# GNN layers on one core: half of the slot additions move from VectorE to TensorE and ScalarE

## Chip, cores and metric

One core of one Trainium2 chip (trn2). The metric is the device time of one execution in microseconds (us). The kernel before takes 6229.18 us, the median of three runs (6227.09, 6229.18 and 6238.08 us).

## What is computed

Four layers of a graph network (GENConv) over 6250 nodes with 64 features and 206,250 edges sorted by their destination. Cut to what matters:

```python
e = edge_attr @ enc_edge_w + enc_edge_b
def _genconv(h, e, src, dst, w1, b1, g1, bb1, w2, b2, t):
    msg = relu(h[src] + e) + EPS_MSG
    m = msg * t
    seg_max = segment_max(m, dst)
    ex = exp(m - seg_max[dst])
    denom = segment_sum(ex, dst)
    agg = segment_sum(msg * ex / (denom[dst] + 1e-16), dst)
    out = h + agg
    z = relu(_layernorm(out @ w1 + b1, g1, bb1))
    return z @ w2 + b2
# layer 0: h = _genconv(h, ...)
# layers 1 to 3: h = h + _genconv(relu(_layernorm(h, ln_g, ln_b)), ...)
```

The change concerns one sum in it: `h[src] + e`, the source's row plus the edge's encoding.

## The kernel before

A first part of some 1770 us encodes the edges and writes their encodings `e` to HBM (`ecell`), placed by destination block and slot. Then come four layers of about 1100 us. `layer` handles the nodes in 49 blocks of 128 destinations, one destination per partition. A block d has 32 slot groups for edges whose sources lie in known blocks, and V[d] overflow slots; every slot is 64 floats wide. Small and large blocks alternate: an odd d has the larger V[d] of its neighbours.

For block d the work is:

- `load_x` (L1243, SP queue): the encodings of all slots of the block into `xb[d % 2]`. It waits for `mul` of block d-2, which reads that buffer last. `load_oh` (L1250, SP queue) brings the one-hot matrices of block d.
- `gathers` (L1258): GpSimd starts V[d] indirect DMAs that bring the sources of the overflow slots into `gb[d % 2]`, after `over` of block d-2.
- `passes(d, j)` for j = 0 to 3 (L1273): TensorE picks the source rows of eight slots by one-hot products in bf16, three parts each, into PSUM bank j. All four together are 147 products of 64 columns. Before it writes a bank it waits for the addition that emptied it (`before_pass`).
- `add(d, j)` (L1290): VectorE adds bank j to the 512 columns of `xb` that hold the encodings of these eight slots, in place.
- `over(d)` (L1302): VectorE adds the gathered rows to the encodings of the overflow slots.
- `most(d)` (L1309, L1313): VectorE takes the maximum over all slots. It waits for all additions of the block.
- `sub` (L1332), the exponential on ScalarE (L1338) and `mul` (L1346): terms of the softmax, in two slices into the ring `ep`; TensorE sums each slice into one bank with products by `ident`, four slots (512 columns, float32) at a time (L1356). `fold` (L1366) reduces that bank on VectorE.
- `node_unit(u)`: for each two blocks, the division, the MLP and the two layer norms. Its steps run through VectorE, ScalarE and TensorE: L1401 hands the sum to TensorE (L1404 to L1411); the first `norm` (L243 to L263) ends in `hb`; L1419 transposes it, L1424 is ScalarE's relu, L1428 the second product, L1432 VectorE's addition to `h`; then comes the second `norm`, and L1439 and L1444 on VectorE read its result.

In `norm`, ScalarE computes the inverse root by Ln and Exp (L246, L248), each with a table load, VectorE refines it (L253, L257, L260), and ScalarE applies it (L263).

The order on every engine is the order in which the loop over d issues the work. Iteration d issues: the gathers of block d+1 on GpSimd and the loads on SP; then for j = 0 to 3 `add(d, j)`, `passes(d + 1, j)` and up to two steps of the node unit under way; `over(d)`, two steps, `most(d)`; `sub`; in an even iteration the steps L1419 to L1428; `fold(d - 1)`; in an odd iteration the start of a new node unit up to the first product; then `mul` with the sums, and further steps. So on TensorE the passes of block d+1 stand behind the sums of block d-1, and L1419 stands behind the passes. The steps of `norm` that wait for ScalarE are spaced by "gap" marks so that the additions stand between them.

At the end of a layer the new rows go to HBM (`ztab`), all engines meet, and the next layer starts. The last layer also fetches `x` rows (L1525) and scatters the output (L1460) on GpSimd.

Of the kernel before, what the change touches and what calls it, by code (L numbers as in the profile page):

```python
# [142 lines left out]
def build(nc, S, T):  # L143
    PE, VE, AE, GP, SP = nc.tensor, nc.vector, nc.scalar, nc.gpsimd, nc.sync
    ND, G = S.ND, S.G
# [5 lines left out]
    with top:  # L151
# [3 lines left out]
        pe_s, ve_s, ae_s = (next(names) for _ in range(3))  # L155
# [5 lines left out]
        def fresh():  # L161

            return Count(pe_s), Count(ve_s), Count(ae_s)
# [7 lines left out]
        def vwait(value):  # L171
            VE.wait_ge(ve_s, value)

        def awaits(engine, *tokens):
            for token in tokens:
                engine.wait_ge(*token)
# [5 lines left out]
        ident, iota, be, prow, base, full, iota1, we = (  # L182
            kept[n] for n in ("ident", "iota", "be", "prow", "base", "full", "iota1", "we"))
# [519 lines left out]
        def sorted_path():  # L703

            with ExitStack() as fc:
# [28 lines left out]
                with nc.Fori(0, S.L - 1) as i:  # L734
                    layer(i, "mid", layer_args)
                layer(S.L - 1, "last", layer_args)

        def lay(z, npd, wri, dci, outi, ovi, yc):
# [461 lines left out]
        def layer(number, tag, args):  # L1200
            (oh, z, h, npd, wri, dci, outi, ovi, xb, gb, mx, top_x, cm, ds, nt, zb, zr) = args
            final = tag == "last"
            P, V, A = fresh()
            lc = ExitStack()
            with lc:
                n_ep, ep_slots = 3, 24
                n_gp = 4
                ep = sb("ep_" + tag, [128, n_ep, ep_slots, 128], FP32, lc)
                xg = zr if final else None
                gps = bank[0:4]  # L1210
# [6 lines left out]
                xg_l = [Landed(s) for s in gq_s[6:8]]  # L1217
                xl_l = [Landed(s) for s in gq_s[8:10]]

                k = {n: {} for n in ("add", "pass", "over", "topx", "sub", "exp", "mul", "sums",  # L1220
                                     "fold", "cm", "node")}
                at = {n: {} for n in ("x", "oh", "g", "xg")}

                def x_of(d, a, b):
                    return xb[d % 2][:, 64 * a:64 * b]

                def slices(d):
                    n = -(-S.S[d] // ep_slots)
                    w = 4 * -(-S.S[d] // (4 * n))
                    return [(a, min(S.S[d], a + w)) for a in range(0, S.S[d], w)]  # L1230
# [31 lines left out]
                def passes(d, j):  # L1262

                    if j == 0 and d >= 2:
                        awaits(PE, at["oh"][d])
                    if (d, j) in before_pass:
                        PE.wait_ge(ve_s, before_pass[d, j])
                    for s in range(8 * j, min(G, 8 * j + 8)):
                        b0, n = S.groups[s]
                        for b in range(b0, b0 + n):  # L1270
                            at_oh = 128 * (S.ones[s] + b - b0)
                            for part in range(3):
                                q = PE.matmul(  # L1273
                                    gps[j % n_gp][:, 64 * (s % 8):64 * (s % 8) + 64],
                                    oh[:, d % 2, at_oh:at_oh + 128],
                                    zp[:, b, 64 * part:64 * part + 64],
                                    start=(b == b0 and part == 0),
                                    stop=(b == b0 + n - 1 and part == 2), skip_group_check=True)
                    k["pass"][d] = P(q)
                    k["pass"][d, j] = k["pass"][d]  # L1280

                before_pass = {}

                def add(d, j):
                    if j == 0 and d:
                        awaits(VE, at["x"][d])
                    VE.wait_ge(pe_s, k["pass"][d, j])
                    lo, hi = 8 * j, min(G, 8 * j + 8)
                    x = x_of(d, lo, hi)
                    k["add"][d] = V(VE.tensor_tensor(x, gps[j % n_gp][:, 0:64 * (hi - lo)], x,  # L1290
                                                     ALU.add))
                    nxt = (d, j + n_gp) if j + n_gp < JS else (d + 1, j % n_gp)
                    before_pass[nxt] = k["add"][d]

                JS = -(-G // 8)

                def over(d):
                    awaits(VE, at["g"][d])
                    if d:
                        awaits(VE, at["x"][d])  # L1300
                    x = x_of(d, G, S.S[d])
                    k["over"][d] = V(VE.tensor_tensor(x, gb[d % 2][:, 0:64 * S.V[d]], x, ALU.add))  # L1302

                def most(d):

                    vwait(max(k["over"][d], k["add"][d]))
                    if d >= 2:
                        VE.wait_ge(ae_s, k["cm"][d - 2])
                    q = V(VE.tensor_reduce(mx[:, 0:64], x_of(d, 0, S.S[d]).rearrange(  # L1309
                        "p (s f) -> p f s", f=64), AX.X, ALU.max))  # L1310
                    yield
                    vwait(q)
                    q = k["topx"][d] = V(VE.tensor_scalar(top_x[:, d % 2, :], mx[:, 0:64], 0.0,  # L1313
                                                          None, ALU.max))
                    u, i = S.where[d]
                    AE.wait_ge(ve_s, q)
                    if u >= 2:
                        AE.wait_ge(ve_s, k["node", "den"][u - 2])
                    q = A(AE.activation(cm[:, u % 2, i, :], top_x[:, d % 2, :], ACT.Exp,  # L1319
                                        scale=nt[:, 0:1]))  # L1320
                    AE.wait_ge(ae_s, q)
                    k["cm"][d] = A(AE.activation(cm[:, u % 2, i, :], cm[:, u % 2, i, :],
                                                 ACT.Identity, scale=npd[:, d:d + 1]))
# [160 lines left out]
                def store_rows(u):  # L1484

                    GP.wait_ge(ae_s, k["node", "rows"][u])
                    for i, d in enumerate(S.units[u]):
                        zs_at[u] = zs_l[u % 2](GP.indirect_dma_start(
                            T["ztab"], bass.IndirectOffsetOnAxis(ap=wri[:, d:d + 1], axis=0),
                            zb[:, u % 2, i, :], None))  # L1490
# [47 lines left out]
                awaits(PE, got_z)  # L1538
                for j in range(JS):
                    passes(0, j)  # L1540
                for d in range(ND):
# [7 lines left out]
                    for u in k["node", "rows"]:  # L1549
                        if u not in zs_at:  # L1550
                            store_rows(u)
                    for j in range(JS):
                        add(d, j)
                        if d + 1 < ND:
                            passes(d + 1, j)
                        steps(2, "normed")
# [4 lines left out]
                    for _ in most(d):  # L1561
                        steps(1, "normed")
                    ready = d and S.where[d - 1][0] != S.where[d][0]
                    steps(99, "end" if ready else "turned")
                    n = len(slices(d))
# [483 lines left out]
```

## Time and profile before

| | |
|---|---|
| Median of three runs | 6229.18 us |
| Profiled execution, its time | 6223.69 us |
| Its span, first to last instruction | 6219.3 us |
| Before the first layer | about 1770 us |
| Mean granted TensorE clock | 0.823 |
| TensorE matmul busy | 4569.7 us |
| VectorE busy | 4590.5 us |
| ScalarE busy | 2451.0 us |
| GpSimd busy | 4260.6 us |

In the rows PE is a TensorE matmul, PEld a TensorE weight load, DVE is VectorE, ACT is ScalarE, POOL is GpSimd and SPq is the queue of SyncE. L1290 is line 1290 of the kernel. A time in brackets behind "idle before" is idle time of that engine right before the instruction, with what ended it. Busy time of DMA-issuing instructions on SP is not counted.

### The profile page before, as it was taken

Reading aid. Unit: us, or ns where it says so; the run is one execution under the profiler, and the core shown is the slowest. Engines: PE = TensorE matmul, PEld = TensorE weight load, DVE = VectorE, ACT = ScalarE, POOL = GpSimd, SP = SyncE. Lnnn points to the kernel's source line nnn. Section 1 sums busy time; section 2 is a strip of 40 time slices with the busy share of each in tenths; the row PEclk is TensorE's granted clock in tenths of the full one; section 3 lists DMA queues with packets and bytes.
Section 4 is the critical chain, followed back from the end, with each engine's and each line's share of the span. In section 5 each row is a group of like instructions: output and inputs, shape, how many; then the busy total and the mean of one; then the engine's idle time right before and its main releaser. Section 6 shows DMA issues by size and latency. Waiting matters only on the chain. (4 is left out here: it accounts for less than half of the span.)

```text
span 6219.3 us, 106998 instructions
## 1 busy us (share of the span) xinstructions
PE 4569.7 (73%) x43557; PEld 3223.3 (52%) x43557; DVE 4590.5 (74%) x7210; ACT 2451.0 (39%) x3848; POOL 4260.6 (69%) x3850
## 2 busy tenths in 40 slices
PE   6715788989937877883877788478878856777776
PEld 6705777888824544452444454245444534444443
DVE  9432555444438999994899999389999948988887
ACT  3403666555513444441334444133443423433333
POOL 3054777766557777774777777477777747777775
PEclk9956988666668998896899889689988978888887
DMA  9962777665565555544555555445555544555452
GB/s 365 416 218 81 255 277 270 230 246 214 190 186 174 177 180 172 185 156 119 169 174 184 176 175 175 119 149 177 180 169 183 183 132 136 172 167 172 158 168 87
DMA packets 323285, 1168.13 MB, mean 188 GB/s; under 512 B 142130, under 2 KB 145380, under 8 KB 255444
## 3 DMA queue, kind: packets, MB, share of 16 engines
q1 hardware_dynamic: 172852, 890.91, 39.1%
q0 software_dynamic: 134800, 214.63, 13.8%
q10 hardware_dynamic: 15120, 55.50, 2.2%
q8 instruction: 352, 5.77, 0.4%
q14 instruction: 161, 1.32, 0.1%
HBM read 910.82 MB, written 249.92 MB: 187 GB/s over the span
## 5 line engine op out<-in xcount | busy, mean ns | idle before, releaser
L1258 POOL DMA_INDIRECT gb<-ztab,ovi x2704 | 2991.3, 1106 | 1009.7 <-issue 826.9
L1356 PE MATMUL bank<-ep_mid,keep 128*128 128x512 f32 (+3 forms) x3474 | 1579.0, 613 | 18.5 <-DVE ep_mid L1346 18.5
L1356 PEld LDWEIGHTS bank<-ep_mid,keep 128*128 128x128 f32 x3474 | 703.8, 204 | 859.3 <-issue 830.2
L1309 DVE TENSOR_REDUCE mx<-xb 128x64 f32<-128x2816 f32 (+17 forms) x196 | 1018.1, 5195 | 3.6
L1273 PE MATMUL bank<-zpw,oh_layers 128*128 128x64 bf16 x28812 | 879.8, 194 | 155.4 <-DMA zpw<-ztab 155.4
L1273 PEld LDWEIGHTS bank<-zpw,oh_layers 128*128 128x128 bf16 x28812 | 874.5, 98 | 210.7 <-DMA zpw<-ztab 156.5
L1096 POOL DMA_INDIRECT ecell<-zpw,ptg x588 | 646.7, 1100 | 227.6 <-issue 177.7
L1404 PE MATMUL bank<-keep,na 128*128 128x128 f32 x100 | 47.5, 475 | 963.1 <-DVE na L1401 963.1
L925 PE MATMUL bank<-byk,zpw 88*88 88x102 f32 (+13 forms) x4608 | 649.5, 327 | 57.8 <-DVE zpw L906 54.1
L925 PEld LDWEIGHTS bank<-byk,zpw 88*88 88x88 f32 (+13 forms) x4608 | 638.0, 229 | 68.9 <-DVE zpw L906 60.3
L1319 ACT ACTIVATE cm<-top_x,nt 128x64 f32<-128x64 f32 x196 | 68.2, 348 | 1505.5 <-DVE top_x L1313 1505.5
L906 DVE TENSOR_TENSOR zpw<-keep,kct 88x440 f32<-88x440 f32 (+13 forms) x468 | 285.3, 631 | 467.4 <-PE bank L925 464.1
L1290 DVE TENSOR_TENSOR xb<-bank,xb 128x512 f32<-128x512 f32 x784 | 510.2, 684 | 107.0 <-PE bank L1273 82.1
L1356 PE MATMUL bank<-ep_last,keep 128*128 128x512 f32 (+3 forms) x1158 | 533.9, 620 | 6.2 <-DVE ep_last L1346 6.2
L1404 PEld LDWEIGHTS bank<-keep,na 128*128 128x128 f32 x100 | 18.2, 182 | 975.4 <-DVE na L1401 975.4
L1338 ACT ACTIVATE ep_mid<-ep_mid,pack 128x1280 f32<-128x1280 f32 (+10 forms) x327 | 444.8, 1390 | 174.9 <-DVE ep_mid L1332 171.7
L1332 DVE SCALAR_TENSOR_TENSOR ep_mid<-xb,top_x 128x1280 f32<-128x1280 f32 (+10 forms) x327 | 484.2, 1527 | 8.8 <-DVE top_x L1313 1.4
L1346 DVE SCALAR_TENSOR_TENSOR ep_mid<-xb,ep_mid 128x1280 f32<-128x1280 f32 (+10 forms) x327 | 489.5, 1524 | 0.5 <-ACT ep_mid L1338 0.5
L1356 PEld LDWEIGHTS bank<-ep_last,keep 128*128 128x128 f32 x1158 | 237.1, 207 | 291.5 <-issue 282.7
L844 ACT COPY bys<-bank 88x325 f32<-88x325 f32 (+11 forms) x468 | 198.6, 424 | 474.6 <-PE bank L925 471.1
L1302 DVE TENSOR_TENSOR xb<-gb,xb 128x768 f32<-128x768 f32 (+17 forms) x196 | 210.5, 1074 | 207.8 <-DMA gb<-ztab,ovi 207.7
L844 ACT COPY byk<-bank 88x512 f32<-88x512 f32 (+10 forms) x306 | 316.0, 1158 | 28.0 <-PE bank L885 27.8
(222 smaller groups left out, 5816.5 us busy)
## 6 DMA issues: line engine op xcount, KB each, us to landing
oh_layers<-ohd SPq DMA_DIRECT2D x196, 1568.0 KB, 9.8
ea_in<-in_ea SPq DMA_DIRECT2D x101, 512.0 KB, 8.4
enc<-es_out ACTq DMA_DIRECT2D x101, 512.0 KB
cb<-rowc SPq DMA_DIRECT2D x49, 1024.0 KB, 5.7
gb<-ztab,ovi POOLq DMA_INDIRECT x2704
ohd<-oh_lay SPq DMA_DIRECT2D x49, 576.0 KB
xb<-ecell SPq DMA_DIRECT2D x20, 1408.0 KB
ohd<-oh_lay SPq DMA_DIRECT2D x49, 512.0 KB
```

The lines of the kernel that those rows point to most:

```text
L844: k["ev"][m] = A(AE.copy(to, src(bank[4 + m % 4])))
L906: k["hot"][g] = V(VE.tensor_tensor(hot[0:kp, g % 3, 0:n, 0:mp], iota1[0:kp, None, 0:mp].broadcast_to([kp, n, mp]), kct[0:kp, a:a + n][:, : ...
L925: q = PE.matmul(b[0:mp, WIDE * j:WIDE * j + WIDE], hot[0:kp, g % 3, j, 0:mp], byk[0:kp, at_d:at_d + WIDE], start=True, stop=True)
L1096: at["sc"][j, h] = sc_l[h](GP.indirect_dma_start(T["ecell"], bass.IndirectOffsetOnAxis(ap=ptg[:, j % 2, e:e + 1], axis=0), prows[:, h, a:a ...
L1258: at["g"][d] = ga_l[d % 2](GP.indirect_dma_start(gb[d % 2][:, 64 * v:64 * v + 64], None, T["ztab"], bass.IndirectOffsetOnAxis(ap=ovi[:, i: ...
L1273: q = PE.matmul(gps[j % n_gp][:, 64 * (s % 8):64 * (s % 8) + 64], oh[:, d % 2, at_oh:at_oh + 128], zp[:, b, 64 * part:64 * part + 64], sta ...
L1290: k["add"][d] = V(VE.tensor_tensor(x, gps[j % n_gp][:, 0:64 * (hi - lo)], x, ALU.add))
L1309: q = V(VE.tensor_reduce(mx[:, 0:64], x_of(d, 0, S.S[d]).rearrange("p (s f) -> p f s", f=64), AX.X, ALU.max))
L1332: k["sub"][d, i] = V(VE.scalar_tensor_tensor(ep[:, r, 0:b - a, 64:128], x_of(d, a, b).rearrange("p (s f) -> p s f", f=64), 0.0, top_x[:, d ...
L1338: k["exp"][d, i] = A(AE.activation(ep[:, r, 0:b - a, 0:64], ep[:, r, 0:b - a, 64:128], ACT.Exp, scale=tcol))
L1346: k["mul"][d, i] = k["mul"][d] = V(VE.scalar_tensor_tensor(ep[:, r, 0:b - a, 64:128], x_of(d, a, b).rearrange("p (s f) -> p s f", f=64), 0 ...
L1356: q = PE.matmul(both[d % 2][:, 0:w], ident, rows[:, 128 * (c - a):128 * (c - a) + w], start=(c == 0), stop=(c + 4 >= S.S[d]), skip_group_c ...
```

## The change

For j = 2 and 3 (`summed`), the passes of a bank begin with a product of `ident` and the 512 columns of encodings in `xb`, in float32, which starts the bank; the one-hot products then accumulate on it. TensorE waits for the load of that block's encodings first. The result is copied back over the encodings in `xb` by ScalarE (the new list `lift`), and VectorE does no addition for these two banks. A bank is free for its next passes when that copy has ended. `most` additionally waits for the last copy of its block. For j = 0 and 1 nothing changes.

```diff
                     if (d, j) in before_pass:
-                        PE.wait_ge(ve_s, before_pass[d, j])
-                    for s in range(8 * j, min(G, 8 * j + 8)):
+                        PE.wait_ge(*before_pass[d, j])
+                    lo, hi = 8 * j, min(G, 8 * j + 8)
+                    if j in summed:
+                        if d:
+                            awaits(PE, at["x"][d])
+                        PE.matmul(gps[j % n_gp][:, 0:64 * (hi - lo)], ident, x_of(d, lo, hi),
+                                  start=True, stop=False, skip_group_check=True)
+                    for s in range(lo, hi):
...
-                                    start=(b == b0 and part == 0),
+                                    start=(b == b0 and part == 0 and j not in summed),
...
                 def add(d, j):
                     if j == 0 and d:
                         awaits(VE, at["x"][d])
-                    VE.wait_ge(pe_s, k["pass"][d, j])
                     lo, hi = 8 * j, min(G, 8 * j + 8)
                     x = x_of(d, lo, hi)
+                    nxt = (d, j + n_gp) if j + n_gp < JS else (d + 1, j % n_gp)
+                    if j in summed:
+                        AE.wait_ge(pe_s, k["pass"][d, j])
+                        k["lift"][d] = A(AE.copy(x, gps[j % n_gp][:, 0:64 * (hi - lo)]))
+                        before_pass[nxt] = ae_s, k["lift"][d]
+                        return
+                    VE.wait_ge(pe_s, k["pass"][d, j])
                     k["add"][d] = V(VE.tensor_tensor(x, gps[j % n_gp][:, 0:64 * (hi - lo)], x,
                                                      ALU.add))
-                    nxt = (d, j + n_gp) if j + n_gp < JS else (d + 1, j % n_gp)
-                    before_pass[nxt] = k["add"][d]
+                    before_pass[nxt] = ve_s, k["add"][d]
 
                 JS = -(-G // 8)
+                summed = (2, 3)
...
                     vwait(max(k["over"][d], k["add"][d]))
+                    VE.wait_ge(ae_s, k["lift"][d])
```

## Rows read from the trace of the kernel before

**Rows 1.** The page's busy times, whole span

```profile
PE 4569.7 (73%) x43557; PEld 3223.3 (52%) x43557; DVE 4590.5 (74%) x7210; ACT 2451.0 (39%) x3848; POOL 4260.6 (69%) x3850
```

**Rows 2.** Busy time by engine in a stretch; the second layer

```profile
2870.00:3970.00 1100.00, 814.76 (x8686) 506.20 (x8686) 938.32 (x1365) 418.46 (x657) 800.43 (x721) 0.86 0.51 164
```

**Rows 3.** VectorE's waits (us, times, longest): second layer, then last layer

```profile
DVE h L1432 <- PE bank L1428: 36.1, 25, 3.8
DVE xb L1302 <- DMA gb<-ztab,ovi: 34.3, 1, 34.3
...
DVE xb L1302 <- DMA gb<-ztab,ovi: 112.0, 20, 34.9
```

**Rows 4.** Groups of instructions by line, whole span

```profile
L1356 PE MATMUL bank<-ep_mid,keep 128*128 128x512 f32 (+3 forms) x3474 | 1579.0, 613 | 18.5 <-DVE ep_mid L1346 18.5
L1290 DVE TENSOR_TENSOR xb<-bank,xb 128x512 f32<-128x512 f32 x784 | 510.2, 684 | 107.0 <-PE bank L1273 82.1 <-DMA xb<-ecell 13.1 <-issue 11.8
L844 ACT COPY byk<-bank 88x512 f32<-88x512 f32 (+10 forms) x306 | 316.0, 1158 | 28.0 <-PE bank L885 27.8
L301 ACT COPY es_out<-bank 128x512 f32<-128x512 f32 x202 | 108.5, 589 | 183.6 <-PE bank L293 164.0 <-DMA enc<-es_out 19.7
```

**Rows 5.** Timeline of blocks 28 to 31, second layer: start, duration, engine, line

```profile
3507.30 4.45 PE L1273 MATMUL bank<-zpw,oh_layers 128*128 128x64 bf16 x147
3513.15 9.45 PE L1356 MATMUL bank<-ep_mid,keep 128*128 128x512 f32 x22
3513.35 0.29 DVE L1432 TENSOR_TENSOR h<-h,bank 128x128 f32<-128x128 f32 x1 [1.22 <-PE bank L1428]
3515.87 0.32 SPq L1243 DMA_DIRECT2D xb<-ecell  x1
3517.34 0.16 DVE L257 SCALAR_TENSOR_TENSOR nwf<-nwf 128x2 f32<-128x2 f32 x1
3518.01 0.15 DVE L260 SCALAR_TENSOR_TENSOR nwf<-mv,nwf 128x2 f32<-128x2 f32 x1
3519.01 0.29 DVE L1439 TENSOR_TENSOR na<-hb,pack 128x128 f32<-128x128 f32 x1 [0.24 <-ACT hb L263]
3520.88 5.52 DVE L1309 TENSOR_REDUCE mx<-xb 128x64 f32<-128x3072 f32 x1
3522.44 4.45 PE L1273 MATMUL bank<-zpw,oh_layers 128*128 128x64 bf16 x147
3534.13 0.29 DVE L1401 TENSOR_TENSOR na<-na,z 128x128 f32<-128x128 f32 x1
3536.45 11.94 PE L1356 MATMUL bank<-ep_mid,keep 128*128 128x512 f32 x24
3540.20 0.20 ACT L248 ACTIVATE nwf<-nwf 128x2 f32<-128x2 f32 x1
3540.44 0.35 DVE L253 SCALAR_TENSOR_TENSOR nwf<-nwf 128x1 f32<-128x1 f32 x2
3542.49 4.84 DVE L1309 TENSOR_REDUCE mx<-xb 128x64 f32<-128x2752 f32 x1
...
3548.23 4.45 PE L1273 MATMUL bank<-zpw,oh_layers 128*128 128x64 bf16 x147
3554.29 0.29 DVE L1432 TENSOR_TENSOR h<-h,bank 128x128 f32<-128x128 f32 x1 [1.26 <-PE bank L1428]
```

**Rows 6.** Stretches: busy PE, PEld, DVE, ACT, POOL; granted clock; DMA share; GB/s

```profile
3524.00:3525.00 1.00, 1.00 (x40) 1.00 (x37) 1.00 (x1) 0.00 (x0) 0.70 (x2) 1.00 0.04 10
...
3529.00:3530.00 1.00, 0.00 (x0) 0.00 (x0) 1.00 (x2) 0.23 (x1) 1.00 (x1) 0.59 0.83 339
...
3913.00:3917.00 4.00, 0.00 (x0) 0.00 (x0) 4.00 (x4) 3.29 (x3) 0.00 (x0) 0.74 0.00 0
```

**Rows 7.** GpSimd's waits (us, times, longest), second layer

```profile
POOL gb L1258 <- DVE zb L1464: 17.9, 8, 7.3
...
POOL gb L1258 <- DVE xb L1302: 3.7, 1, 3.7
```

More of the change, by code:

```diff
@@ L1218, in layer @@
                 xl_l = [Landed(s) for s in gq_s[8:10]]
-                k = {n: {} for n in ("add", "pass", "over", "topx", "sub", "exp", "mul", "sums",
+                k = {n: {} for n in ("add", "lift", "pass", "over", "topx", "sub", "exp", "mul", "sums",
                                      "fold", "cm", "node")}
```

## Prediction

> **What bounds the kernel now.** I read the page's busy times first. VectorE is busy 4590 us and TensorE 4570 us of 6219 [rows 1]: two engines are equally full, so no share tells which one a piece of work should be taken from. The first 1770 us are untouched by the change. In one layer VectorE is busy 938 of 1100 us, TensorE 815 and GpSimd 800 [rows 2]. VectorE looks like the bound, but its waits say where it is not: in each of 25 node units it stops at L1432 for TensorE's L1428, 36.1 us per layer [rows 3]. The decisive view is the timeline of two neighbouring blocks, which repeats 23 times in a layer [rows 5]. It splits into two halves.
>
> *Half B*, from L1432 at 3513.35 to the end of L1401 at 3534.42: 21.07 us. VectorE runs here almost without a break. TensorE does the sums (9.45 us), then the 147 passes (4.45), and is through at 3526.89; it then idles 7.6 us until L1401 hands it the node sum.
>
> *Half A*, from 3534.42 to the next L1432 at 3554.29: 19.87 us. TensorE does the node's products, the sums of the larger block (11.94 us from 3536.45), the passes from 3548.23 to 3552.68, then L1419, and after ScalarE's L1424 the product L1428. VectorE needs that result and has waited 1.26 us. So half A is TensorE's: whatever is put into its queue ahead of L1419 delays L1432, and only half B is VectorE's.
>
> **The change, part by part.**
>
> *Removed:* two of four additions per block at 0.684 us [rows 4], 1.37 us per block of VectorE, 2.74 per pair, 268 us over 196 blocks.
>
> *Added on TensorE:* two identity products of 512 float32 columns per block. The trace has the same kind in the sums: 43 slots make 11 products, shown as 22 records in 9.45 us [rows 5], so 0.43 us per record and 0.86 per product. (The 613 ns of [rows 4] is the length of one record; records overlap, so the spacing is the price.) Two are 1.72 us per block. They stand in the passes, which take the same 4.45 us in both halves, at the full clock of half B's (1.00 [rows 6]). The bounds: 1.7 us where all is hidden but the stream, 1.9 with a float32 weight load that the short bf16 products ahead can't hide. I take 1.72.
>
> *In half A* these 1.72 us lie on the path to L1432 (the passes of the next block stand ahead of L1419): +1.72 us. What VectorE gains in this half comes to nothing, since it arrives earlier at the same wait. That gain is small anyway: L253 waits for ScalarE's L248, which ends at 3540.40 [rows 5], whether three additions or two stand ahead of it.
>
> *In half B* the 1.72 us come ahead of TensorE's 7.6 us of idle time, which shrinks to about 5.4: cost nothing. If that cover went, the next late thing would be L1404. VectorE drops two additions. The chain of the second norm needs them as cover: L257 ends at 3517.50; L260 followed at 3518.01 because an addition stood between, and can now follow at about 3517.54. L1439 came 1.00 us after L260 because it waits for ScalarE's L263 [rows 5]; the addition that stood in this gap goes, and the gap stays. So L1439 and all behind it come 0.47 us earlier, not 1.37. Bounds: 0.2 if a copy delays L263, 1.37 if the gap could be filled. I take 0.47.
>
> *Added on ScalarE:* two copies out of PSUM per block. The nearest row is L301, same shape, 0.589 us; the helper's copies at L844, with 88 partitions and strided output, took 1.16 [rows 4]. I take 0.59. In block order one copy stands behind L248 and the next ahead of or behind L263. In half B the second copy ends near 3519.1 (L1439's old start), and `most`, the first to need it, started at 3520.88 and can now at 3520.4: hidden, even at 1.16 us. In half A the copies follow L248 and end at 3540.40 + 1.18 = 3541.6, before `most` at 3542.49 less up to 0.5: hidden too, and at 1.16 us up to 0.8 us late, which falls into VectorE's wait at L1432. Over the layer ScalarE goes from 418 us busy by 58 us.
>
> *New waits.* TensorE waits for the load of the encodings at its third bank. In half A the load is issued after the two `mul` that follow L1401, some 10 us before the passes begin. In half B it is issued at 3515.87; the DMA engines are empty by 3524 (share 0.04) [rows 6]; the third bank would start after 51 of 147 passes, 3522.44 + 1.54 = 3523.98. This is tight, but a stall here of up to 5 us falls into TensorE's idle time. The wait of the passes for the copies of the block before is met 4 us or more earlier in both halves. SP and GpSimd issue nothing new and stand behind no new wait; the gathers of block d+1 still wait for `over` of d-1. VectorE's wait for the last copy is costed above.
>
> *Clock.* In the idle time of half B the granted clock falls from full to half (2.4 to 1.2 GHz) after 2.3 us (0.59 in 3529 to 3530 [rows 6]), and the first sums of half A run at half rate. With 5.4 us idle I expect the same fall: in the shorter idle stretch of 4.2 us near 3913 it fell too (mean 0.74 [rows 6]). So no gain and no loss.
>
> *Sum.* Per pair +1.72 − 0.47 = +1.25 us. Half A with passes behind its sums occurs in blocks 2, 4, ... 46: 23 per layer, and half B as often. Three layers: 69 × 1.25 = +86 us. At a layer's start the extra products are hidden by the one long wait for the gathered rows of block 1 (34.3 us [rows 3]). In the last layer VectorE waits 20 times for the gathered rows (112.0 us [rows 3]), GpSimd having more to issue there: about 4 to 5 us per pair from block 13 on, which swallows both the 1.25 us of each pair and the 7 us gathered before. I take 0 for it; bounds 0 to +8.
>
> The sum is made on the profiled execution, 6223.7 + 86 = 6310 us; the median of the runs stands 5.5 us above it, so 6315 us.
>
> **The rivals.**
>
> *R1, VectorE bounds throughout: faster.* If L1432's wait could be absorbed elsewhere, each pair would gain up to 2.74 us, 63 per layer. GpSimd caps this: within a layer it waits only 17.9 + 3.7 us for VectorE [rows 7], otherwise it issues without a break, so a layer can't shrink by more than some 25 us. Time: 6229 − 3 × 25 = 6154 us. For it speaks VectorE's larger busy time; against it, the 25 waits at L1432. It decides if TensorE's half A is 1.3 us or more shorter than I read it. Chance 0.08.
>
> The Trainium skill (Perfetto Trace Analysis, "Identifying the Most-Contended Engine") would have one find the engine with the highest occupancy and relieve it first. By that VectorE is relieved and the time falls as in R1. The waits in this case's trace speak against it.
>
> *R2, the clock stays up: slightly faster.* If 5.4 us of idle time with a load's stall in it no longer lets the clock fall, half A's sums run at 0.43 us per record from the start: 24 × 0.43 = 10.3 instead of 11.94 us, −1.6 per pair. Net −0.35 × 69 = −24: 6205 us. Against it, the fall after 2.3 us. Chance 0.05.
>
> The Trainium skill (TensorE: Matmul & The Clock Gate, "Loop structure matters more than you think") says that back-to-back matmuls keep the clock up and long waits lose it. A denser TensorE queue would by this rule lean to R2; the 4.2 us row says that this change is not dense enough.
>
> *R3, no change.* The addition to half A is offset by 1.2 us: L1424 and L1428 close up, or the pair's rhythm falls well against the clock. Time 6229. Chance 0.05.
>
> *R4, slower by more.* The lifted products run at the half clock (1.72 more), or the copies delay L263 and so L1439, or the load stalls TensorE beyond its idle time. One of them per pair adds about 0.8 to 1.7 us: 69 × 2.0 to 3.0 = 138 to 207, 6367 to 6436 us. Against it: half A's passes now take no longer than half B's, and half B has cover. Chance 0.10.
>
> **How the numbers follow.** My case has 0.72. Its own ends: +0.35 per pair (B gains 1.37) gives 24 us, 6253; 1.9 on TensorE and 0.2 gained, with 8 in the last layer, gives 125 us, 6354. The range needs 8 in 10, so it goes up a little into R4: 6250 to 6370. A measurement can tell about 0.2% (12 us) from no change. Faster: R1 and R2, 0.13. Same: R3, 0.05. Slower: my case and R4, 0.82.
>
> **What would show it.** Right: L1290 ×392; VectorE's wait at L1432 grows from 1.5 to about 3.4 us each in the first three layers, about +45 us per layer; TensorE's passes last about 6.2 us; the wait of L1439 for ScalarE grows to about 0.9; the two-block period goes from 40.9 to about 42.2 us in the first three layers and stays about 44 late in the last, with shorter waits for gathered rows. Wrong: waits at L1432 that stay near 1.2 us, a clock that doesn't fall between L1273 and L1404, or VectorE waiting for gathered rows in the middle layers, which would be GpSimd as the new bound.

## Result and profile after

The changed kernel takes 6320.59 us (median of four runs, 6313.32 to 6323.0) against 6228.14 us: a ratio of 1.0151, 95% interval 1.0128 to 1.0175, so 92 us slower. The prediction was 6315 us.

The page's busy times of the changed kernel (in the order of [rows 1]):

```profile
PE 4941.6 (78%) x44340; PEld 3369.7 (53%) x44341; DVE 4368.9 (69%) x6818; ACT 2629.8 (42%) x4240; POOL 4294.0 (68%) x3850
```

VectorE lost 222 us of work and the kernel became slower. The new groups by line; L1272 is the identity product, L1298 ScalarE's copy, L1302 the addition that stays:

```profile
L1272 PE MATMUL bank<-xb,keep 128*128 128x512 f32 x784 | 449.3, 656 | 133.4 <-DMA xb<-ecell 132.4
...
L1302 DVE TENSOR_TENSOR xb<-bank,xb 128x512 f32<-128x512 f32 x392 | 252.2, 684 | 101.7 <-PE bank L1279 85.8 <-DMA xb<-ecell 15.9
...
L1298 ACT COPY xb<-bank 128x512 f32<-128x512 f32 x392 | 214.3, 572 | 213.5 <-PE bank L1279 213.5
```

VectorE's waits in the second layer of the changed kernel (us in total, times, longest), to be read against [rows 3]. L1445 is the old L1432, L1314 the old L1302, L1452 the old L1439:

```profile
DVE h L1445 <- PE bank L1441: 83.3, 25, 5.6
DVE xb L1314 <- DMA gb<-ztab,ovi: 40.2, 3, 39.3
...
DVE na L1452 <- ACT hb L263: 21.0, 25, 0.8
DVE nwf L253 <- ACT nwf L248: 18.0, 26, 1.8
```

The wait for TensorE's L1441 rose from 36.1 to 83.3 us. That growth of 47 us exceeds the loss of a layer, some 25 us: it contains what VectorE gained by arriving earlier. The timeline of the same blocks as in [rows 5] shows both halves. L1279 is the passes (three pieces of 51, 48 and 48), L1369 the sums, L1414 the old L1401:

```profile
3569.54 0.29 DVE L1445 TENSOR_TENSOR h<-h,bank 128x128 f32<-128x128 f32 x1 [4.18 <-PE bank L1441]
...
3578.62 1.65 PE L1279 MATMUL bank<-zpw,oh_layers 128*128 128x64 bf16 x51
...
3580.94 1.10 PE L1272 MATMUL bank<-xb,keep 128*128 128x512 f32 x2 [0.67 <-DMA xb<-ecell]
...
3589.62 0.29 DVE L1414 TENSOR_TENSOR na<-na,z 128x128 f32<-128x128 f32 x1
...
3591.64 11.88 PE L1369 MATMUL bank<-ep_mid,keep 128*128 128x512 f32 x24
...
3595.93 0.35 DVE L253 SCALAR_TENSOR_TENSOR nwf<-nwf 128x1 f32<-128x1 f32 x2 [0.59 <-ACT nwf L248]
...
3603.36 1.65 PE L1279 MATMUL bank<-zpw,oh_layers 128*128 128x64 bf16 x51
3604.85 1.10 PE L1272 MATMUL bank<-xb,keep 128*128 128x512 f32 x2
3605.79 1.56 PE L1279 MATMUL bank<-zpw,oh_layers 128*128 128x64 bf16 x48
3607.19 1.10 PE L1272 MATMUL bank<-xb,keep 128*128 128x512 f32 x2
3608.13 1.56 PE L1279 MATMUL bank<-zpw,oh_layers 128*128 128x64 bf16 x48
3611.30 0.29 DVE L1445 TENSOR_TENSOR h<-h,bank 128x128 f32<-128x128 f32 x1 [3.21 <-PE bank L1441]
3616.47 0.29 DVE L1452 TENSOR_TENSOR na<-hb,pack 128x128 f32<-128x128 f32 x1 [0.84 <-ACT hb L263]
```

The two halves as stretches (columns as in [rows 6]):

```profile
3569.54:3589.91 20.37, 15.57 (x173) 9.07 (x172) 18.21 (x31) 8.89 (x16) 16.11 (x15) 1.00 0.60 205
3589.91:3611.30 21.39, 20.89 (x189) 11.91 (x190) 17.28 (x22) 9.68 (x15) 17.12 (x15) 0.92 0.45 144
```

Half B went from 21.07 to 20.37 us, half A from 19.87 to 21.39. In half A TensorE is busy 20.89 of 21.39 us. The passes last from 3603.36 to 3609.69, 6.33 us in place of 4.45.

Over the 69 pairs of the first three layers in which half A has passes, worked out from the starts of the two additions to `h` and the ends of the node sums: half A grew by 1.6 us on average (20.1 to 21.7), half B shrank by 0.5 (21.2 to 20.7). From block 1's maximum to block 48's a layer takes 996 to 1004 us (971 to 975 before). That is 77 of the 96 us that part the two profiled executions. The last layer's blocks add 3.5, the edges of the layers 3. The other 12 us lie ahead of the first layer, in code that the change doesn't touch: the first gather starts at 1761.2 instead of 1748.9. In the profiled executions of these two kernels and of the first four experiments it lies between 1748.0 and 1761.2, and one kernel with the products starts as early as the kernel before; so the change is not needed for a late start. Whether the other three executions of the changed kernel have these 12 us too was not recorded.

### The profile page after: what moved, and what is told of

Same layout as the page of the kernel before. It is cut to its first block and busy times, and to the rows that moved or that the text cites. A ratio compares the mean times of both kernels' runs of the same rounds, so it can differ in the third digit from the quotient of the medians.

```text
span 6315.7 us, 108957 instructions
## 1 busy us (share of the span) xinstructions
PE 4941.6 (78%) x44340; PEld 3369.7 (53%) x44341; DVE 4368.9 (69%) x6818; ACT 2629.8 (42%) x4240; POOL 4294.0 (68%) x3850
## 5 line engine op out<-in xcount | busy, mean ns | idle before, releaser
L1258 POOL DMA_INDIRECT gb<-ztab,ovi x2704 | 3033.5, 1122 | 1063.5 <-issue 828.7
L1369 PE MATMUL bank<-ep_mid,keep 128*128 128x512 f32 (+3 forms) x3474 | 1555.8, 606 | 0.0
L1279 PEld LDWEIGHTS bank<-zpw,oh_layers 128*128 128x128 bf16 x28812 | 938.9, 99 | 446.3 <-issue 274.8
L1369 PEld LDWEIGHTS bank<-ep_mid,keep 128*128 128x128 f32 x3474 | 692.5, 202 | 829.0 <-issue 794.2
L1279 PE MATMUL bank<-zpw,oh_layers 128*128 128x64 bf16 x28812 | 954.0, 194 | 156.2 <-DMA zpw<-ztab 156.2
L1272 PE MATMUL bank<-xb,keep 128*128 128x512 f32 x784 | 449.3, 656 | 133.4 <-DMA xb<-ecell 132.4
L1369 PE MATMUL bank<-ep_last,keep 128*128 128x512 f32 (+3 forms) x1158 | 523.2, 610 | 0.6 <-DVE ep_last L1359 0.6
L1369 PEld LDWEIGHTS bank<-ep_last,keep 128*128 128x128 f32 x1158 | 232.5, 203 | 279.4 <-issue 267.2
L1314 DVE TENSOR_TENSOR xb<-gb,xb 128x768 f32<-128x768 f32 (+17 forms) x196 | 210.8, 1075 | 202.5 <-DMA gb<-ztab,ovi 202.3
```

Of the source, the lines that this page charges most:

```text
L1258: at["g"][d] = ga_l[d % 2](GP.indirect_dma_start(gb[d % 2][:, 64 * v:64 * v + 64], None, T["ztab"], bass.IndirectOffsetOnAxis(ap=ovi[:, i: ...
L1272: PE.matmul(gps[j % n_gp][:, 0:64 * (hi - lo)], ident, x_of(d, lo, hi), start=True, stop=False, skip_group_check=True)
L1279: q = PE.matmul(gps[j % n_gp][:, 64 * (s % 8):64 * (s % 8) + 64], oh[:, d % 2, at_oh:at_oh + 128], zp[:, b, 64 * part:64 * part + 64], sta ...
L1369: q = PE.matmul(both[d % 2][:, 0:w], ident, rows[:, 128 * (c - a):128 * (c - a) + w], start=(c == 0), stop=(c + 4 >= S.S[d]), skip_group_c ...
```

## Experiments

The first four ran against a kernel before of 6226.3 us (median of 13). Lines in the expectations are those of the kernel before, L1314 excepted.

**Only even blocks, only odd blocks.** The rule that picks the banks looks at the block too; both kernels compute all of it.

```diff
-                summed = (2, 3)
+                def lifts(d, j):
+                    return d % 2 == 0 and j in (2, 3)   # second kernel: d % 2 == 1
```

> Only even blocks take the identity products and the copies. Their passes are issued in odd iterations, ahead of TensorE's idle time (half B), and their copies fall into half A, where VectorE waits for TensorE anyway. My theory (the products cost only where they stand ahead of L1419 in half A, VectorE gains only in half B): 0 +- 10 us against the kernel before, 6228, and the wait at L1432 of the second layer grows only by what VectorE gains, from 1.5 to about 1.9 us each. Rival, the cost is spread over all products (slower engines through more work on TensorE and ScalarE): half of the change's loss, +46. Rival, VectorE's removed additions count wherever they are: -25 to -50.

> Only odd blocks take the products and the copies. Their passes stand in half A, ahead of L1419 (+1.72 us per pair), their copies in half B (-0.47). My theory: the whole loss of the change, +86 to +92, so 6314 to 6320. Rival, the cost is spread evenly: +46.

Measured: even 6218.19 us (0.9982, interval 0.9972 to 0.9991), odd 6310.11 us (1.0137, 1.0118 to 1.0156). Nearly the same number of products, copies and removed additions (24 blocks of a layer are odd, 25 even) costs 84 us in one place and gains 8 in the other. This rules out a cost spread over all products, and it rules out VectorE's removed additions as a gain wherever they are. The profiled executions agree: blocks 1 to 48 of the first three layers together take 72 us longer with odd blocks and 4.5 us less with even ones. VectorE's wait for the second product in the second layer (36.1 us before), even blocks, then odd:

```profile
DVE h L1448 <- PE bank L1444: 45.9, 25, 3.8
```

```profile
DVE h L1448 <- PE bank L1444: 73.1, 25, 5.6
```

With even blocks it grows by 9.8 us (0.4 each), what VectorE gains in half A and can't use. With odd ones half A is 1.5 us longer and half B 0.5 shorter, close to the changed kernel. The even kernel is also a little faster than the kernel before, at the edge of what can be told. Its blocks 1 to 48 take 0.8 us more in the first layer and 2.3 and 3.0 less in the next two; the profiled execution is the slowest of its ten (6227.4 us), so where the 8 us are gained is not shown.

**The product left out.** The encodings of 16 of the 32 slot groups are not added; the wait for the load and the copies stay.

```diff
-                        PE.matmul(gps[j % n_gp][:, 0:64 * (hi - lo)], ident, x_of(d, lo, hi),
-                                  start=True, stop=False, skip_group_check=True)
...
-                                    start=(b == b0 and part == 0 and j not in summed),
+                                    start=(b == b0 and part == 0),
```

> As the changed kernel, but the identity product is left out: the encodings of 16 of the 32 slot groups are not added, TensorE does the 147 products alone (its wait for the load stays), ScalarE copies as before. My theory: TensorE's +1.72 us in half A goes, VectorE's -0.47 in half B stays: -32 us, 6196. The wait at L1432 stays near 1.9 us. If VectorE were the bound throughout: -75 (GpSimd then caps it). If the copies or the new waits were the cost and not the product: it stays near 6310.

Measured: 6256.15 us (1.0044, 1.0027 to 1.0061). 64 us less than the changed kernel, but 30 more than before, where 32 less were expected. Half A did return to 20.1 us (before 20.1). Half B did not stay short: it takes 21.6 us (before 21.2). The rest is a bound that I had put too far away. VectorE's waits in its second layer:

```profile
DVE xb L1312 <- DMA gb<-ztab,ovi: 57.2, 9, 38.2
DVE h L1443 <- PE bank L1439: 51.2, 25, 3.8
```

VectorE waits for gathered rows nine times instead of once. Up to block 29 the layer gained 3.6 us on the kernel before; from there to block 48 it lost 13. The gathers themselves were slower: a gather of blocks 2 to 48 took 1.14 us on average in this layer, 1.11 before, 17 us over 637 of them. The traces show where. A gather takes 0.94 us (the median) while no `scalar_tensor_tensor` of VectorE runs, and 1.26 on average (up to 2.51) in the kernel before when it meets one. But this is not what changed: in the second layer gathers and these instructions coincide for 273 us, 274 before. What changed is the meeting with the overflow addition, L1312 here, whose two operands both lie in SBUF. Before, 52 gathers of the layer overlap it and take 1.01 us on average; here 66 do, and take 1.23. Above 0.94 each, that is 15 of the 17 us. One of them:

```profile
3084.82 1.48 DVE L1312 TENSOR_TENSOR xb<-gb,xb 128x1280 f32<-128x1280 f32 x1
...
3085.22 1.90 POOL L1258 DMA_INDIRECT gb<-ztab,ovi  x1 [0.30 <-issue]
```

The changed kernel has 54 such gathers of 1.18 us on average. Fewer additions on VectorE let the overflow addition start earlier, but that this alone makes more gathers fall into it, and that the slower gathers are all of the 30 us, is argued and not shown.

**Copies by VectorE.**

```diff
-                        AE.wait_ge(pe_s, k["pass"][d, j])
-                        k["lift"][d] = A(AE.copy(x, gps[j % n_gp][:, 0:64 * (hi - lo)]))
-                        before_pass[nxt] = ae_s, k["lift"][d]
+                        VE.wait_ge(pe_s, k["pass"][d, j])
+                        k["add"][d] = V(VE.tensor_copy(x, gps[j % n_gp][:, 0:64 * (hi - lo)]))
+                        before_pass[nxt] = ve_s, k["add"][d]
...
-                    VE.wait_ge(ae_s, k["lift"][d])
```

> As the changed kernel, but VectorE makes the copies out of PSUM in place of ScalarE: VectorE then has as many instructions of the same shape as before, and TensorE the added products. My theory: +1.72 us per pair from TensorE and nothing gained in half B: 69 x 1.72 = +119, 6347; if a copy is shorter than the 0.684 us addition by a tenth, some 5 us less. Rival, ScalarE's copies are a cost of the change (they delay L263 or the maximum): then this is no slower than the changed kernel, 6320 or less.

Measured: 6335.07 us (1.0181, 1.0159 to 1.0204), 109 us slower than before, where 119 were expected. VectorE's copies by line, to be read against L1302 in the groups above (684 ns):

```profile
L1298 DVE COPY xb<-bank 128x512 f32<-128x512 f32 x392 | 266.2, 682 | 37.8 <-PE bank L1279 31.6 <-issue 6.2
```

A copy costs VectorE as much as the addition. Half B is back at 21.1 us (20.7 in the changed kernel, 21.2 before) and half A stays at 21.7. So half B's gain comes from taking the work off VectorE, and ScalarE's copies cost nothing that these halves show; the intervals of this kernel and of the changed one overlap, so it is the halves and not the totals that show it.

**A period of slower execution.** The runs that follow fell, on three chips, one of them the chip of the four runs above, into a time in which the kernel before took 8404 to 8580 us. So each is compared only with the kernel before that ran beside it. The traces show TensorE stopping within the passes for no wait that they name ("issue"). TensorE's largest wait from 2300 us on, in the kernel of the next paragraph with the fourth group:

```profile
PE bank L1279 <- issue: 1387.6, 2106, 60.0
```

What stopped it is not known. In that kernel half A takes 37 us and half B 21 in the first three layers: TensorE's passes weigh much more than in the profile of before. The kernel before itself has no trace from this period.

**One slot group at a time.** `j in (2, 3)` becomes `j == 3`, and `j == 2`.

> Only the fourth slot group (j = 3) of every block. TensorE +0.86 us in half A. VectorE's fourth addition stood between L260 and L1439, where VectorE waits for ScalarE's L263 for 1.00 us anyway, so taking it out gains nothing: 0. My theory: 69 x 0.86 = +59 us, 6287, and the wait at L1439 goes from 0.24 to about 0.9 us. Rival, each removed addition gains its 0.684 us in half B: +0.18 per pair, +12.

> Only the third slot group (j = 2) of every block. TensorE +0.86 us in half A; the third addition stood between L257 and L260, so L260 comes 0.47 us earlier, and the fourth addition still fills the wait for L263. My theory: 69 x 0.39 = +27 us, 6255. Both banks gain alike if it is not the place in the norm's chain that counts: then the same time as with the fourth group alone.

Measured: fourth group 8467.52 us (1.0064, 1.0029 to 1.0099), third 8438.72 us (1.0022, 0.9993 to 1.0051), before 8413.42. The order is as expected (the fourth costs more, 54 and 25 us by the medians, 59 and 27 forecast), but the intervals overlap, and the times alone don't decide. VectorE's wait for the second norm does. In the second layer, fourth group, then third (L1455 is the old L1439):

```profile
DVE na L1455 <- ACT hb L263: 21.0, 25, 0.8
```

```profile
DVE na L1455 <- ACT hb L263: 7.2, 25, 0.8
```

In the profile of before this wait was 7.2 us too. Without the fourth addition it grows to 0.84 us each (0.9 forecast); without the third it stays at 0.24, and half B is 0.45 us shorter than with the fourth removed. So it is the place in the norm's chain that counts: the time that the fourth addition gives back goes into the wait, and half B's gain comes from the third.

**Later passes.** In even iterations the passes of the next block leave the places ahead of L1419. All outputs are computed.

```diff
-                        if d + 1 < ND:
+                        if d + 1 < ND and d % 2:
                             passes(d + 1, j)
...
                     steps(99, "end" if ready else "turned")
+                    if d + 1 < ND and d % 2 == 0:
+                        for j in (0, 1):
+                            passes(d + 1, j)
                     n = len(slices(d))
                     for i in range(n):
                         sub(d, i)
                     steps(99, "linear2")
+                    if d + 1 < ND and d % 2 == 0:
+                        for j in (2, 3):
+                            passes(d + 1, j)
```

Applied to the kernel before:

> The kernel before, with one order changed: in even iterations the passes of the next block are issued behind L1419 (two banks) and behind L1428 (two banks), no longer ahead of both. My theory: TensorE's half A ends 4.45 us sooner, L1432 no longer waits, and half A becomes VectorE's: -1.2 us per pair, more in blocks 2 to 10 where the wait was up to 3.8: about -34 us per layer of the first three, but GpSimd's gathers cap it at some -25: -60 to -90 in all, about 6155. If the wait at L1432 had another cause (ScalarE's part), no change.

Measured: 7905.65 us against 8413.42 (0.9415, 0.9376 to 0.9454). Applied to the changed kernel:

> The changed kernel with the same later passes in even iterations. The two added products no longer stand ahead of L1432, so half A costs nothing for them and VectorE's shorter work counts in both halves (-0.45 and -0.47). My theory: at least as fast as the kernel before with the same order, 6135 to 6155, held there by GpSimd's gathers, with VectorE waiting at the overflow addition (L1314) in the later half of every layer. TensorE's idle time in half B nearly vanishes (7.6 - 4.6 - 1.7 and less), so the clock may stay up. Rival, the products cost wherever they stand (TensorE total, 36 of 39 us per pair): 6228 or more.

Measured: 7985.22 us (0.9505, 0.9468 to 0.9543). Both were run twice more.

> Again the kernel before with its passes of even iterations behind L1419 and L1428, after a run on a chip where every kernel takes a third longer. On a chip like that of the profile, my theory: the wait at L1432 (36 us per layer before) shrinks to below 15, and the time falls by what GpSimd's gathers allow. The kernel without the product showed them as the next bound, so less than I took for this at first: -20 to -70 us, 6155 to 6205. If the wait at L1432 is not TensorE's queue: 6226.

> Again the changed kernel with the later passes. My theory: the products stand in TensorE's idle time in both halves, the loss of the change (+92) goes, and the time is that of the kernel before with the same order within 20 us, held by GpSimd's gathers. Rival, TensorE's total counts: it stays 60 us or more above the kernel before with the same order.

> The kernel before with its passes of even iterations behind L1419 and L1428, tried a third time for a chip on which the kernel before takes some 6226 us. There: the wait at L1432 shrinks to below 15 us per layer and the time falls by 20 to 70 us, to 6155 to 6205, held by GpSimd's gathers; 6226 if the wait at L1432 is not TensorE's queue. On a chip like the last two: 0.943 of the kernel before again.

> The changed kernel with the later passes, the same. Where the kernel before takes 6226 us: within 20 us of that kernel with the same order, as the products then stand in TensorE's idle time; rival, TensorE's total counts, and it stays 60 us or more above it. On a chip like the last two: 0.951 again, so some 60 us above.

Measured: 7934.4 (0.9430, 0.9382 to 0.9477) and 7996.06 us (0.9509, 0.9464 to 0.9553) against 8404.25; 8151.0 (0.9512, 0.9467 to 0.9556) and 8219.53 us (0.9582, 0.9531 to 0.9633) against 8579.89. The slower period lasted, so how much the order gains outside it, the 20 to 70 us expected, was not measured. In it the last pair gained less than the 0.943 and 0.951 expected of it.

What they show is the mechanism. VectorE's waits for the second product from 2300 us on, in the kernel with the fourth group alone (passes ahead of it), and in the kernel before with later passes ("remote" is a releaser that the trace doesn't name):

```profile
DVE h L1448 <- PE bank L1444: 687.4, 90, 15.4
```

```profile
DVE h L1432 <- PE bank L1428: 73.9, 87, 4.3
...
DVE h L1432 <- remote: 47.1, 13, 10.2
```

Passes that no longer stand ahead of it bring this wait from 687 to 121 us (the two kernels also differ by the fourth group's product). The kernel with the products is 62 to 80 us slower than the one without, in the same order. By the times, then, my expectation (within 20 us, or faster) failed, and the rival's number came (60 us or more above). The traces tell where. In the first pair of kernels blocks 1 to 48 of the first three layers take as long with the products (1252 to 1254 us) as without (1243 to 1261); in the second likewise, in the third with the products 3 to 19 us less. The difference arises at the layers' start, in all three pairs: from block 0's maximum to block 1's it takes 28 to 42 us with the products, 16 to 18 without, and block 0's maximum itself comes 5 to 11 us later after the first gather. In the second layer of the changed kernel with later passes, for block 1:

```profile
3731.40 2.05 PE L1272 MATMUL bank<-xb,keep 128*128 128x512 f32 x2 [10.09 <-DMA xb<-ecell]
...
3750.34 7.74 DVE L1322 TENSOR_REDUCE mx<-xb 128x64 f32<-128x4544 f32 x1 [15.10 <-issue]
```

TensorE's first product waits 10.1 us for the load of the block's encodings, a wait that the plain passes don't have; its last passes come behind the sums, and ScalarE's copy of them ends 0.1 us before the maximum starts. So in the repeated pairs the products stand in idle time as I had expected, and at the layers' start they don't. The rival's reason, TensorE's total, is not what the traces show.

## Why the prediction was right

- *VectorE's additions are not the bound where they are removed, L1432's wait is.* Confirmed: the wait grew by 47 us in the second layer, 45 were forecast, and the kernel with odd blocks alone is 84 us slower, where the whole change costs 92.
- *Identity products, 1.72 us per block in half A.* Measured 1.88: 0.94 from a product's start to that of the passes behind it, where the sums' spacing had given 0.86. The upper bound was 1.9.
- *A stall for the load in half B falls into TensorE's idle time.* It did: 0.67 us in the pair shown, and TensorE still idles 4.2 us behind it.
- *Clock: no gain and no loss.* A small gain instead. In the pair shown TensorE idles 4.2 us, and the clock is still full (1.00) to the end of half B; it falls only after TensorE has resumed. A clock that doesn't fall between L1273 and L1404 was one of my signs of being wrong. It came in 20 of the 69 pairs, in two of which the clock doesn't fall at all; in the other 49 it fell in the idle time as forecast. What it is worth is small: in half A TensorE runs 3.9 us at half clock on average instead of 4.6, and half A's growth is 1.88 − 0.28 = 1.60 us, with 0.28 from an earlier first sum and shorter sums. This 0.28 is the term that I had put at nothing. By the Trainium skill's rule (TensorE: Matmul & The Clock Gate, "Loop structure matters more than you think") back-to-back matmuls keep the clock up, so a denser queue leans to R2. The traces bear that out only in part. With even blocks alone TensorE's idle time shrinks as well (7.9 to 5.3 us), yet its time at half clock stays (4.7 us); with odd blocks alone the idle time hardly shrinks (7.4 us), and the time at half clock is 4.0 us. So the gain came with the products in half A, for a reason that no run here shows, and it is far from R2's 1.6 us.
- *Half B, −0.47 us.* Measured −0.46 on average, −0.70 in the pair shown. L1439's wait went from 0.24 to 0.84 us (0.9 forecast), as the fourth group alone shows too. In half A, L253 got a new wait of 0.59 us in the pair shown: the removed additions had covered both.
- *The sum of +1.25 per pair.* Half A and B give +1.1; over three layers 77 us, against 86. The products cost more than I took, and the clock gave back more than that. That 6315 us lies so near to 6320.59 is partly luck: the profiled execution has 12 us ahead of the first layer that are not the change's, and 6 us in the last layer and at the layers' edges.
- *The last layer absorbs it.* Yes: +3.5 us between blocks 1 and 48.
- *R1's cap by GpSimd, 25 us per layer,* was too wide: without the product VectorE waits for gathers already, and the layer is longer than before. The Trainium skill's advice (Perfetto Trace Analysis, "Identifying the Most-Contended Engine") is to optimize the engine with the highest occupancy first. Within a layer VectorE was that engine, and relieving it gained 8 us with even blocks alone and nothing without the product: VectorE relieved, TensorE's work as before, and 30 us slower.

## What to carry over

Where two engines alternate as the bound within one period, cut the period at the waits and price a change in each half by itself: the same two products cost 84 us over the kernel where another engine's wait stands behind them, and nothing where TensorE idles behind them. An instruction that fills the time of a wait for another engine gains nothing when it is removed; the wait takes its place. Before work is moved to an engine, look at what stands behind it in that engine's queue and who waits for that; the order may be worth more than the work.

## What the runs showed of the hardware

- VectorE took the same 0.68 us for a copy of 512 float32 columns out of PSUM as for the addition of PSUM and SBUF; ScalarE took 0.57.
- A gather's issue on GpSimd, 0.94 us, took 1.26 us on average, at most 2.5, when it met a `scalar_tensor_tensor` of VectorE, up to 1.9 when it met an addition of two SBUF operands (in the kernel without the product), and still 0.94 when it fell wholly within the long `tensor_reduce`.
- The same kernel took 6226 us and, later on the same chip, 8580 us. In that later time TensorE stopped within runs of small products in every kernel traced, while one such product took as long as before (0.193 us). A comparison holds only between runs made together.
